# Windowed attention on one Trainium2 core: two query blocks a step, one column-tiled burst, normalised ahead of the transposition

## The reference

```
q, k, v = split(layernorm(x) @ w_qkv)         # 16 heads of 32, windows of 128
k_ctx, v_ctx = the window before, its own and the one after
scores = (q * 32**-0.5) @ k_ctx.T             # 128 x 384, out-of-range keys masked
out = softmax(scores) @ v_ctx
```

## Time and profile before

| | |
|---|---|
| median of three runs | 3324.11 us |
| the profiled execution | 3329.27 us, its span 3327.5 us |
| attention, from its first score to its last DVE instruction | about 605 to 1455 us of the span |
| busy over the whole span | PE 93%, PEld 73%, DVE 66%, ACT 37%, POOL 24% |
| mean granted TensorE clock | 0.964 of full speed |

### The profile page before, as it was taken

The page is one execution under the profiler, slowest core; times in us unless marked ns, Lnnn a source line. Parts: engine busy times, 40 slices in busy tenths (PEclk is TensorE's granted clock), DMA queues, the critical chain, the costliest instruction groups (busy, mean ns, idle before and its releaser), DMA issues. The chain is left out here.

```text
span 3327.5 us, 60152 instructions
## 1 busy us (share of the span) xinstructions
PE 3090.0 (93%) x20536; PEld 2426.7 (73%) x20536; DVE 2212.5 (66%) x4354; ACT 1215.8 (37%) x1970; POOL 791.2 (24%) x625
## 2 busy tenths in 40 slices
PE   7999999799999999959987999879999999989998
PEld 6888888577777777737766777658877787878886
DVE  4333332487877878758758878777786858597633
ACT  2222222355555555545532222222232323322232
POOL 0000000477777777753310000110001000010011
PEclk9999999799999999979988999989999999999999
DMA  5455454565666656659979999879795969688632
GB/s 190 164 186 186 158 196 157 137 165 157 166 164 160 163 160 163 164 175 341 369 291 404 403 399 397 302 260 348 285 356 209 349 220 341 248 316 303 215 119 72
DMA packets 439988, 795.24 MB, mean 239 GB/s; under 512 B 28080, under 2 KB 160176, under 8 KB 439864
## 3 DMA queue, kind: packets, MB, share of 16 engines
q1 hardware_dynamic: 439872, 793.73, 69.9%
HBM read 600.16 MB, written 192.94 MB: 238 GB/s over the span
## 5 line engine op out<-in xcount | busy, mean ns | idle before, releaser
L1418 DVE SCALAR_TENSOR_TENSOR e_part<-ring,e_g_cols,e_part 128x512 f32<-128x512 f32 x896 | 634.4, 771 | 38.1 <-DMA ring<-mix_rows 38.1
L644 DVE TENSOR_REDUCE b_neg_max<-b_ps_score 128x1 f32<-128x384 f32 (+1 forms) x1024 | 521.9, 539 | 187.9 <-PE b_ps_score L519 177.8
L1362 ACT ACTIVATE e_u<-e_hid,e_mb 128x512 f32<-128x512 f32 x256 | 176.5, 689 | 969.8 <-PE e_hid L1310 969.6
L1324 PE MATMUL e_acc<-e_w_hi,e_u_hi 128*128 128x512 f32 x1024 | 419.7, 410 | 105.5 <-DVE e_u_lo L1428 105.5
L1269 POOL TENSOR_TENSOR e_rows<-e_rows,e_prev 128x512 f32<-128x512 f32 x64 | 95.7, 1525 | 1501.2 <-DVE e_rows L1456 998.3
L1325 PE MATMUL e_acc<-e_w_lo,e_u_hi 128*128 128x512 f32 x1024 | 412.9, 403 | 0.0
L1326 PE MATMUL e_acc<-e_w_hi,e_u_lo 128*128 128x512 f32 x1024 | 411.8, 402 | 0.0
L1308 PE MATMUL e_hid<-e_y_hi,e_w_hi 128*128 128x512 f32 x1024 | 401.5, 392 | 10.5 <-DMA e_y_lo<-yl_scratch 8.2
L519 PE MATMUL b_ps_score<-b_k_st,b_q_st 96*128 96x384 f32 (+1 forms) x1024 | 390.2, 389 | 20.0 <-DMA b_k_st<-qk_scratch 18.2
L1309 PE MATMUL e_hid<-e_y_lo,e_w_hi 128*128 128x512 f32 x1024 | 400.4, 391 | 0.0
L1310 PE MATMUL e_hid<-e_y_hi,e_w_lo 128*128 128x512 f32 x1024 | 400.1, 391 | 0.0
(11 more groups left out here) (113 smaller groups left out, 4958.7 us busy)
## 6 DMA issues: line engine op xcount, KB each, us to landing
ring<-mix_rows SPq DMA_DIRECT2D x576, 512.0 KB, 7.8
qk_scratch<-a_qk SPq DMA_DIRECT2D x128, 512.0 KB, 2.7
b_q_st<-qk_scratch SPq DMA_DIRECT2D x192, 256.0 KB, 3.1
b_k_st<-qk_scratch SPq DMA_DIRECT2D x192, 256.0 KB, 3.4
e_y_hi<-yh_scratch SPq DMA_DIRECT2D x40, 1024.0 KB, 9.6
e_y_lo<-yl_scratch SPq DMA_DIRECT2D x40, 1024.0 KB, 11.9
part_scratch<-e_rows SPq DMA_DIRECT2D x24, 1024.0 KB, 6.8
e_prev<-part_scratch SPq DMA_DIRECT2D x24, 1024.0 KB, 10.4
```

The source lines that it names most:

```text
L644: dve.tensor_reduce(neg_max[:, m % 2, h:h + 1], ps_score[:, h % 2, 0:(hi - lo) * WIN], AX_X, ALU.max, negate=True).then_inc(reduced, 1)
L1324: pe.matmul(acc[t][:, :], u_hi[:, s % 2, cols], w_hi[:, slot, D:2 * D], start=begin, stop=False)
L1418: dve.scalar_tensor_tensor(out=part[:, n % 2, cols], in0=ring[:, i % RING, cols], scalar=g_cols[:, b, e:e + 1], in1=so_far, op0=ALU.mult, ...
```

## The change

Only `phase_attention` changes. A step now serves a pair of neighbouring query blocks; there are 128 pairs, and all steps are written out, without a hardware loop.

- Scores: two heads share one buffer and one wait; `ps_score` has two buffers of two heads, and DVE reduces 128 x 2 x 384 to 128 x 2 at once. Four reductions a pair instead of eight.
- Maxima: the eight of a pair are transposed and copied together; the row DMAs stay two a pair.
- Keys: each head has its own wait and its own exponential (128 x 384), with two buffers of one head.
- Values and sums of both blocks: one unbroken burst of 24 and 8 column-tiled matmuls into one PSUM bank.
- Normalisation: DVE takes the reciprocal of the sums and multiplies right on the burst's result, before the transposition. The sums stand there as 128 partitions (head and feature) x 256 queries, so both operations are 256 columns wide. PE then transposes two tiles instead of four, and ACT copies them out.
- POOL: the same four additions a pair, two of them in another order.
- SP: the first round loads all four chunks ahead of the first row; later loads go by keys and queries apart; a store goes out per pair.

```diff
-    AHEAD, TURN_M, PV_LAG, OUT_LAG = 4, 3, 2, 3
-    RING = 4
+    HALF = W // 2
+    PAIRS = ROUNDS * HALF
+    AHEAD, LAG = 3, 2
+    RING = 8
...
-        ps_score = psum("ps_score", [P, 2, 512])
-        ps_keys = [psum(f"ps_keys{i}", [P, 2, 512]) for i in range(2)]
-        ps_out = psum("ps_out", [P, 512])
-        ps_turn = psum("ps_turn", [P, 512])
+        inv_sum = sb("inv_sum", [P, 2 * WIN], F32)
+        out_t = sb("out_t", [P, 2, 2 * WIN], F32)
+        out = sb("out", [P, 2, 2, QH * E], F32)
+        ps_score = [psum(f"ps_score{i}", [P, 2, 512]) for i in range(2)]
+        ps_keys = [psum(f"ps_keys{i}", [P, 512]) for i in range(2)]
+        ps_out = psum("ps_out", [P, 4, WIN])
+        ps_turn = psum("ps_turn", [P, 4, WIN])
...
+        STEPS = range(-AHEAD, PAIRS + LAG + 1)
...
-                for c in range(3):
-                    load(0, c)
+                for c in range(4):
+                    load_k(0, c)
+                    load_q(0, c)
+                for c in range(4):
+                    load_v(0, c)
+                for T in STEPS:
...
+                    if there(T - LAG - 1):
+                        store(T - LAG - 1)
+                    if there(T + AHEAD - 1):
+                        row(T + AHEAD - 1)
...
+                def score(g, s):
...
+                    if y >= 2:
+                        pe.wait_ge(reduced, y - 1)
+                    for a in range(2):
+                        h = 2 * pair + a
+                        mm = pe.matmul(ps_score[y % 2][:, a, 0:(hi - lo) * WIN], q_st[0:STACK, h, w * WIN:(w + 1) * WIN],
+                                       k_st[0:STACK, h, lo * WIN:hi * WIN], start=True, stop=True)
...
+                def keys(g, x):
...
+                    if x >= 2:
+                        pe.wait_ge(exp_done, x - 1)
...
+                def values(g):
...
+                    if g >= 1:
+                        pe.wait_ge(norm_done, g)
...
+                for T in STEPS:
+                    for s in range(2):
+                        if there(T + AHEAD):
+                            score(T + AHEAD, s)
+                    for x in range(2):
+                        if there(T):
+                            keys(T, x)
+                    if there(T - LAG):
+                        values(T - LAG)
+                        sums(T - LAG)
+                    if there(T + AHEAD - 1):
+                        turn_max(T + AHEAD - 1)
+                    for x in range(2, 4):
+                        if there(T):
+                            keys(T, x)
+                    for s in range(2, 4):
+                        if there(T + AHEAD):
+                            score(T + AHEAD, s)
+                    for x in range(4, 8):
+                        if there(T):
+                            keys(T, x)
+                    if there(T - LAG):
+                        turn_out(T - LAG)
...
+                    act.activation(probs[:, m % RING, h, 0:(hi - lo) * WIN], ps_keys[x % 2][:, 0:(hi - lo) * WIN],
+                                   ACT.Exp, scale=SCALE).then_inc(exp_done, 1)
...
+                def normalise(g):
+                    dve.wait_ge(pv_done, g + 1)
+                    dve.reciprocal(inv_sum[:, :], ps_out[:, 2:4, :].rearrange("p w q -> p (w q)")).then_inc(inv_done, 1)
+                    dve.wait_ge(inv_done, g + 1)
+                    if g >= 2:
+                        dve.wait_ge(out_turned, g - 1)
+                    dve.tensor_tensor(out_t[:, g % 2, :], ps_out[:, 0:2, :].rearrange("p w q -> p (w q)"), inv_sum[:, :],
+                                      ALU.mult).then_inc(norm_done, 1)
...
+                for T in STEPS:
+                    for s in range(2):
+                        if there(T + AHEAD):
+                            reduce(T + AHEAD, s)
+                    if there(T - LAG):
+                        normalise(T - LAG)
+                    if there(T + AHEAD - 1):
+                        copy_rows(T + AHEAD - 1)
+                    for s in range(2, 4):
+                        if there(T + AHEAD):
+                            reduce(T + AHEAD, s)
```

More of the change, by code:

```diff
@@ L391, in span, with there, threes @@
             return max(w - 1, 0), min(w + 2, W)
[L393 to L401, removed]
+        def there(g):
+            return 0 <= g < PAIRS
+        STEPS = range(-AHEAD, PAIRS + LAG + 1)
+        def threes(m):
+            return sum(0 < v % W < W - 1 for v in range(m + 1))
         with nc.Block() as block:
@@ L405, in _, with tokens @@
             def _(sp):
[L406 to L420, removed]
+                def tokens(n, c):
+                    return slice(n * SEQ + c * CH, n * SEQ + (c + 1) * CH)
@@ L455, in _, with load_q @@
[L455 to L465 removed]
+                def load_q(n, c):
+                    load_stack(n, c, q_st, 0, (0, 1, 0), q_loaded)
@@ L466, in _ @@
                 for s in out_stored:
-                    sp.wait_ge(s, 16 * (1 + 2 * ROUNDS))
+                    sp.wait_ge(s, 16 * (PAIRS // 2))
             @block.gpsimd
@@ L618, in copy_out @@
-                def copy_out(n, m):
-                    act.wait_ge(pv_done, 4 + W * n + m + 1)
-                    act.activation(out_t[:, m % 2].rearrange("p a q -> p (a q)"), ps_out[:, 0:2 * WIN],
-                                   ACT.Copy).then_inc(out_copied, 1)
-                def step(n, j, there):
-                    for pair in range(2):
-                        if there(j):
-                            weights(n, j, pair)
-                    if there(j - PV_LAG):
-                        copy_out(n, j - PV_LAG)
@@ new lines, in copy_out @@
+                def copy_out(g):
+                    act.wait_ge(out_turned, g + 1)
+                    if g >= 2:
+                        act.wait_ge(out_stored[g % 2], 16 * (g // 2))
+                    act.activation(out[:, g % 2].rearrange("p w e -> p (w e)"),
+                                   ps_turn[:, 1:3, :].rearrange("p w e -> p (w e)"), ACT.Copy).then_inc(out_copied, 1)
+                for T in STEPS:
+                    for x in range(2):
+                        if there(T):
+                            weights(T, x)
+                    if there(T - LAG - 1):
+                        copy_out(T - LAG - 1)
+                    for x in range(2, 8):
+                        if there(T):
+                            weights(T, x)
```

301 lines of the change are left out of this document (143 added, 158 removed).

## The result

The kernel after takes 3413.21 us (median of 4 runs, 3410.72 to 3413.91); the kernel before, run beside it, 3326.01 us (3323.9 to 3334.18). The ratio is 1.0256, 95% interval 1.0237 to 1.0275: slower by 2.6%. The forecast was 3382 us, with a range of 3275 to 3430. In the profiled executions it is 3413.91 against 3329.27, 84.6 us more, and 83.5 of it are there by attention's last VectorE instruction (1455.55 before, 1539.09 after): the projection takes the same time in both within 0.2 us, the phases behind attention within 0.9.

What follows compares the result with a forecast made beforehand. PE's issue bounds attention before; the change closes a PE–DVE loop, 6.85 us a pair against 6.50. 3329.3 + 44 + 8 = 3381, or 3376 for the median, set slightly higher at 3382 us; range 3275 to 3430.

Steps and rivals of the forecast that it cites:

- The ring: PE and DVE in attention: burst, normalisation, copy of maxima, two reductions, two scores, next burst in a row; 6.97 us a pair.
- Steps 1 and 7: Hand-over from the sums' end to DVE, 0.06 us, and PE's merged burst of values and sums, 1.96 us.
- Step 2: DVE's reciprocal of 128 x 256 at six column-times of a reduction: 1.69 us, or 1.4 to 2.0.
- Rival 2: DVE's reciprocal costs eight column-times, 8.2 ns: 2.24 us, the pair 7.40, the whole 3445 us; chance 0.10.
- Steps 3 and 4: On DVE: gap 0.03 and multiply 0.43 us, then copy of maxima and two reductions, 1.90 us.
- Step 6: On PE: two scores and two keys behind an uncovered weight load, then entry to the burst; 0.84 us.
- the loop: The ring between PE and DVE: 6.85 us a pair with short blocks against 6.50, adding 44 us.
- The start: First row of maxima waits in SP's queue behind 28 loads instead of 21: 8 us more.
- the tail: Three more steps without scores at the end in either kernel: 0 ± 3 us.
- Rival 1: Reciprocal streams like a reduction, 0.43 us, and the loop through ACT binds: 6.10 a pair, 3282 us; chance 0.26.
- the exponentials' ring: The loop through ACT's exponentials and PE's keys, to bind if the reciprocal is short: 6.22 us, less 0.12.
- Rival 3: PE's savings are real and the loop isn't tight: −25 to +25 us around the forecast, within its own range.

Runs made afterwards that it cites:

- e1_copy: The kernel after with its 128 x 256 reciprocal replaced by a copy of the same size, so output is not normalised; 3263.79 us, 0.9822 of before.
- e2_half: The kernel after with a reciprocal of the first block's sums only (128 x 128), used for both blocks; 3299.67 us, 0.9927 of before.
- e7_fill: The kernel after with four extra useless transpositions a pair on TensorE, two ahead of each of the first two scores; 3397.61 us, 1.022 of before.
- e4_split: The kernel after with the transposition of the maxima put between values and sums, cutting the burst in two; 3489.24 us, 1.0502 of before.
- e3_start: The kernel after with 18 loads instead of 28 ahead of the first rows of maxima, ten issued behind them; 3408.8 us, 1.0251 of before.
- f7_start: A reordered kernel normalising behind the transposition (3290.24 us), changed to 18 start loads first and ten behind the third pair's rows; 3278.64 us, 0.9867 of before.

## Why the prediction was right in sign and short in size

The ring is the one that was forecast, and so is the reason for the slowdown: e1_copy and e2_half move the time by the reciprocal alone. By its steps:

- Steps 1 and 7 (hand-over and burst): 2.02 forecast, 2.03 measured (1003.31 to 1005.34 with the start of the load; 1.89 to the next load).
- Step 2 (the reciprocal): 1.69 forecast, 1.757 measured. With 173 ns at four columns that is (1757 − 173) / 252 = 6.29 ns a column where 6 was taken, and e2_half's 957 ns lies on the same line within 5 ns. The assumption that decided the sign, that the cost is in the columns and not in the fixed part, held. That 6 came so near owes something to luck: it hung on which other operation's fixed part was borrowed, 149 or 138 ns, and the rows then on record allowed anything from 1.02 to 8.75 ns a column. The Trainium skill (VectorE: DVE Perf Modes, section "First, the fixed hardware budget") gives reciprocal a repeat count of 8. Read as eight column-times of a reduction, which is an estimate and not the page's word, that would be 8.2 ns, and the measurement does not agree: it is 6.2 of them. Rival 2 is dead by that.
- Steps 3 and 4 (multiply, copy, two reductions): 2.33 forecast from the multiply's start (0.43 + 1.90), 2.34 measured, from 1007.13 to the end of the second reduction at 1009.47, which stands 0.05 ahead of the load at 1009.52:
```profile
1008.53 0.94 DVE L650 TENSOR_REDUCE b_neg_max<-b_ps_score 128x2 f32<-128x768 f32 x1
```
- Step 6 (two scores, two keys, entry): 0.84 forecast, 0.91 measured (1009.52 to 1010.43).
- Their sum: 6.97 forecast, 7.11 measured; with the short blocks 6.85 and 6.96. Before was 6.48 on the mean, where one round of the earlier trace rows had given 6.50. So the loop costs 0.475 × 125 = 59 us, not 44. Steps 2 and 6 are what was taken too small, by 0.07 each.
- The start: 8 forecast, 7.7 measured.
- Not in the sum: the ten stretches at half clock, 14.2 us by the spans of after and e7_fill (3411.9 and 3397.7). 59 + 8 + 14 is 81 of 84.6 us; of the last 3 or so, 0.9 lie in the phases behind attention, and the rest, within the ±3 left to the tail, was not followed up.
- What the ring hid: that TensorE alone would need 5.1 us a pair. No run shows it. In e1_copy, whose exponentials set the pace, TensorE has a matmul in flight for 44.95 us of a round (windows view), 5.6 a pair:
```profile
1003.00:1050.05 47.05, 44.95 (x649) 36.16 (x648) 35.61 (x57) 29.44 (x72) 37.50 (x31) 1.00 0.78 181
```
But the plain round of after, with the same matmuls, has 49.28, 6.2 a pair. So time in flight grows with the waits and only bounds the work from above. Before has 6.45 by this count, and what the merging saves of TensorE's own work, 1.4 us a pair or less, stays open. It cost the forecast nothing, since the ring was longer.

Rival 1 had the right successor (the exponentials' ring), but its condition, a reciprocal under 1.3 us, didn't hold; where a run makes it hold, the sign does change (e2_half, 0.96 us, and e1_copy, 0.43 us, are both faster than before). Rival 3's ±25 was meant for a loop that isn't tight; the loop was tight, and the miss of 31 us is half the ring (15) and half the clock (14).

## What to carry to other kernels

Before an operation is moved ahead of a transposition, count its columns on both sides: the reciprocal went from 4 columns a block to 256 a pair, and an operation that is cheap at 4 (0.17 us) is not at 256 (1.76 us). When work is regrouped into larger steps, write down the ring that two in-order engines form through each other's buffers, with every instruction between the wait and the release: here that gave the time of a pair within 2%. And when a change leaves TensorE idle in many short waits, read the granted clock in windows of some microseconds, since the mean over a phase (0.98) hides it.

## What the runs showed of the hardware that was not expected

- Reciprocal on VectorE, 128 partitions, float32: 173 ns for 4 columns, 957 for 128, 1757 for 256; a copy of the same 256 columns takes 425.
- TensorE at 1.2 GHz for 3.41 us at a time in the middle of a stream whose longest time without a matmul in flight is 0.5 us (without a weight load 0.71): 8 times in some 800 us of after, 31 in some 950 us of e4_split's rounds, 0 in before and in e7_fill, where the waits are filled with matmuls of no use.
- Cutting one column-tiled burst in two inside the ring, with a short transposition between its parts, cost 0.33 us a pair at full clock (e4_split).
- A small transfer waits in its queue behind the loads issued ahead of it: with seven more loads in front the first row of maxima is issued 12.6 us later, and in e3_start ten loads put between two pairs' rows stop the keys for 7.1 us. Behind the third pair's rows (f7_start) they stop nothing for long.
